# Third dense tap and paired image halves in a chain of four convolution blocks

## The reference

```python
# block 0: masked, grouped (4 groups)
out = relu(_gconv(x * m1, w1, 0))                 # 1x1, 256 -> 64
out = relu(_gconv(out * m2, w2, 1)) * m2          # 3x3, 64 -> 64
x = relu(_gconv(out, w3, 0) + x)                  # 1x1, 64 -> 256
# block 1: modulated deformable convolution
out = relu(group_norm(conv(x, w1)))               # 256 -> 64
om = conv(out, w_off, pad=1) + b_off              # 27 maps: 9 dx, 9 dy, 9 mask
sampled = bilinear_sample(out, py, px) * sigmoid(mask)    # 9 taps per pixel
out = einsum("bckhw,ock->bohw", sampled, w2)
out = relu(group_norm(out))
x = relu(group_norm(conv(out, w3)) + x)
# block 2: the same with biases in place of the norms and without modulation (18 maps)
# block 3: theta, phi, g = 1x1 of x to 16 channels (plus biases)
f = theta^T phi / N;  y = f g;  wy = conv1x1(y, w_w)
out = batch_norm(wy) + x
```

## Time and profile before

| | us |
|---|---|
| median of 3 runs (264.29 to 270.0) | 269.53 |
| the profiled execution | 269.83 |
| its span | 268.0 |
| busy: PE, DVE, ACT, POOL | 210.7, 158.3, 117.9, 136.0 |
| granted TensorE clock, mean | 0.877 of full |

### The profile page before, as it was taken

The page is one execution under the profiler, slowest core; times in us unless marked ns, Lnnn a source line. Parts: engine busy times, 40 slices in busy tenths (PEclk is TensorE's granted clock), DMA queues, the critical chain, the costliest instruction groups (busy, mean ns, idle before and its releaser), DMA issues. The chain is left out here.

```text
span 268.0 us, 2403 instructions
## 1 busy us (share of the span) xinstructions
PE 210.7 (79%) x808; PEld 109.6 (41%) x808; DVE 158.3 (59%) x270; ACT 117.9 (44%) x159; POOL 136.0 (51%) x127
## 2 busy tenths in 40 slices
PE   8999987787979568196997979489876764999920
PEld 7364963543333223034873746233332231343500
DVE  2965537766867954844166466567476676352271
ACT  2120335786686837001206148848738551023231
POOL 6000017877878877870010077788777787720010
PEclk9999995678899999677799975979899998699965
DMA  7400113323233232230000223223323223310004
GB/s 257 171 0 2 39 41 98 98 86 93 80 99 93 83 98 80 79 98 21 0 2 0 78 66 110 78 83 95 98 78 97 81 80 97 100 39 0 0 0 157
DMA packets 8654, 19.80 MB, mean 74 GB/s; under 512 B 1985, under 2 KB 4162, under 8 KB 8514
## 3 DMA queue, kind: packets, MB, share of 16 engines
q0 software_dynamic: 5376, 14.69, 18.0%
q1 hardware_dynamic: 3122, 4.44, 4.8%
q10 hardware_dynamic: 144, 0.52, 0.5%
HBM read 17.55 MB, written 2.10 MB: 73 GB/s over the span
## 5 line engine op out<-in xcount | busy, mean ns | idle before, releaser
L321 POOL DMA_INDIRECT G<-table,idx x112 | 129.1, 1153 | 58.1 <-issue 47.7
L558 DVE TENSOR_TENSOR GW<-G,corner_w 128x1024 f32<-128x1024 f32 (+1 forms) x32 | 34.9, 1091 | 52.0 <-DMA G<-table,idx 51.1
L951 PE MATMUL ps<-first,GS 128*128 128x128 f32 x64 | 15.5, 328 | 37.1 <-DVE GS L573 37.0
L753 ACT ACTIVATE sT<-ps 128x256 f32<-128x256 f32 x32 | 12.2, 381 | 64.0 <-PE ps L951 64.0
L906 PE MATMUL ps<-x,V 128*64 128x512 f32 x64 | 38.4, 731 | 0.0
L723 ACT ACTIVATE near_y<-ps,dbias 128x1024 f32<-128x1024 f32 x32 | 35.4, 1106 | 1.5 <-PE ps L898 1.5
L308 POOL TENSOR_TENSOR rstd<-var,half_neg 64x1 f32<-64x1 f32 (+1 forms) x4 | 2.6, 638 | 64.0 <-DVE var L371 42.2
L726 ACT ACTIVATE hat_y<-near_y 128x1024 f32<-128x1024 f32 x32 | 33.8, 1057 | 1.0
L799 PE MATMUL ps<-first 128*128 128x128 f32 x180 | 28.6, 316 | 0.0
L799 PEld LDWEIGHTS ps<-first 128*128 128x128 f32 x180 | 25.7, 224 | 4.2 <-issue 3.9
L951 PEld LDWEIGHTS ps<-first,GS 128*128 128x128 f32 x64 | 7.1, 153 | 45.0 <-DVE GS L573 43.7
(11 more groups left out here) (132 smaller groups left out, 235.1 us busy)
## 6 DMA issues: line engine op xcount, KB each, us to landing
G<-table,idx POOLq DMA_INDIRECT x112, 2.9
second<-in_second SPq DMA_DIRECT2D x1, 1552.5 KB, 8.6
table<-feat_t SPq DMA_DIRECT2D x4, 256.0 KB, 2.3
out<-x SPq DMA_DIRECT2D x4, 256.0 KB, 2.2
x<-in_x ACTq DMA_DIRECT2D x1, 512.0 KB, 4.6
x<-in_x SPq DMA_DIRECT2D x1, 512.0 KB, 5.4
first<-in_first SPq DMA_DIRECT2D x1, 224.0 KB, 4.4
at_w<-in_w_b SPq DMA_DIRECT2D x1, 1.0 KB
```

The lines of the kernel that those rows point to most:

```text
L321: pool.indirect_dma_start(out=G[:, done % RING, k, :], out_offset=None, in_=table[b], in_offset=bass.IndirectOffsetOnAxis(ap=idx[b][:, n:n ...
L558: dve.tensor_tensor(GW[:, :, k0:k1].rearrange("p c k e -> p k c e"), G[:, (b * TILES + t) % RING, k0:k1].rearrange("p k (c e) -> p k c e", ...
L753: act.activation(sT[:, t % 2, 2 * part:2 * part + 2], ps[:, B_ST[part], 0:2 * P] .rearrange("p (q n) -> p q n", n=P), ACT.Copy).then_inc(s ...
L951: mm = pe.transpose(ps[:, B_ST[part], q % 2 * P:(q % 2 + 1) * P], GS[:, t % 2, k:k + 2, :].rearrange("p k e -> p (k e)"), ident)
```

## The change

Nine taps are split 3 dense and 6 gathered. The second part of a tile has two taps, one pair, so 48 gathers a layer. A dense chunk isn't |.| then 1-|.| then times hat_x, but one `scalar_tensor_tensor`, min(|y distance|, 1) * hat_x; since hat_y = 1 - min(|.|, 1), the contribution is VS·hat_x - V·S, where VS is the sum of V over the tiles. So V is stored negated, and for each tap one matmul pair with VS is added. Line 726 goes; near_y becomes the ring, of 4. V of the third tap is in bank 7.

The 64-channel results of half 0 stand in partitions 0 to 63 and those of half 1 in 64 to 127 of one bank (`side(h)`): conv1, dense and contraction write the two halves to different columns of the array, conv3 reads them from different rows. hid is 128x512. conv3 waits for both halves; QUARTERS is ordered by slab, and the norms of 64 channels read 128 partitions in one bn_stats.

```diff
-DENSE = 2
+DENSE = 3
+PART_PAIRS = [range(0, 2), range(2, PAIRS)]
-BESIDE = [0, 0, 1, 1, 2, 1, 1, 2, 1, 1, 2, 1, 1, 2, 0, 0]
+BESIDE = [0, 0, 2, 1, 3, 2, 2, 2, 2, 2, 2, 2, 2, 1, 1, 0]
-PREPARE = [(-1, -1, -1), (3, FIRST_TAP_ENDS - AHEAD, 5)]
-HRING = 3
+PREPARE = [(-1, -1, -1)] + [(end - AHEAD - 1, end - AHEAD, end - AHEAD) for end in TAP_ENDS]
+HRING = 4
...
-        hid = 3 * [sb("hid", [HID, N])]
+        hid = 3 * [sb("hid", [P, HALF])]
...
+        def side(h):
+            return slice(h * HID, (h + 1) * HID)
...
-        QUARTERS = [(h, m) for h in range(2) for m in range(CT)]
+        QUARTERS = [(h, m) for m in range(CT) for h in range(2)]
+        OUT_QUARTERS = [(h, m) for h in range(2) for m in range(CT)]
... DVE
+            def weigh(b):
+                dve.wait_ge(s_V, 3 * b + 3)
+                dve.tensor_scalar(V2[:].rearrange("p t e -> p (t e)"), ps[:, B_V2, :], -1.0, None,
+                                  ALU.mult).then_inc(s_weigh, 1)
+                dve.tensor_reduce(VS[:, 2], ps[:, B_V2, :].rearrange("p (t e) -> p e t", e=HID),
+                                  mybir.AxisListType.X, ALU.add).then_inc(s_weigh, 1)
+                dve.tensor_scalar(V[:].rearrange("p t d e -> p (t d e)"),
+                                  ps[:, B_V:B_V + 2, :].rearrange("p h n -> p (h n)"), -1.0, None,
+                                  ALU.mult).then_inc(s_weigh, 1)
+                dve.tensor_reduce(VS[:, 0:2].rearrange("p d e -> p (d e)"),
+                                  ps[:, B_V:B_V + 2, :].rearrange("p h (t e) -> p e (h t)", e=2 * HID),
+                                  mybir.AxisListType.X, ALU.add).then_inc(s_weigh, 1)
...
-                    dve.wait_ge(s_hy, cd + 1)
+                    dve.wait_ge(s_ny, cd + 1)
...
-                    dve.tensor_tensor(S[cd % SRING], hat_y[cd % HRING], hat_x[:, c // TILES],
-                                      ALU.mult).then_inc(s_S, 1)
+                    dve.scalar_tensor_tensor(out=S[cd % SRING], in0=near_y[:, cd % HRING], scalar=1.0,
+                                             in1=hat_x[:, c // TILES], op0=ALU.min,
+                                             op1=ALU.mult).then_inc(s_S, 1)
... ACT
-                act.wait_ge(s_ny, cd + 1)
-                act.activation(hat_y[cd % HRING], near_y[:, c % 2], ACT.Relu,
-                               scale=-1.0, bias=1.0).then_inc(s_hy, 1)
... PE
             def conv1(b, weights, src, ready):
-                for h in range(2):
-                    for t in range(CT):
-                        pe.wait_ge(ready[t], h + 1)
-                        mm = pe.matmul(ps[0:m, B_C1 + h, :], weights[:, t, :], half(src[:, t, :], h),
+                for t in range(CT):
+                    for h in range(2):
+                        pe.wait_ge(ready[h], t + 1)
+                        mm = pe.matmul(ps[side(h), B_C1, :], weights[:, t, :], half(src[:, t, :], h),
                                        start=(t == 0), stop=(t == CT - 1))
...
             def conv3(b, weights, start):
-                for h in range(2):
-                    pe.wait_ge(s_hid[b], h + 1)
-                    for m in range(CT):
-                        pe.matmul(quarter(m, h), weights[:, m * P:(m + 1) * P], half(hid[b], h),
+                pe.wait_ge(s_hid[b], 2)
+                for m in range(CT):
+                    for h in range(2):
+                        pe.matmul(quarter(m, h), weights[side(h), m * P:(m + 1) * P], hid[b][side(h)],
                                   start=start, stop=True).then_inc(s_c3[b], 1)
... positions
+                                if i == 0:
+                                    pe.wait_ge(s_weigh, 4 * b + 2)
... dense(c)
+                    i, t = divmod(c, TILES)
+                    if t == 0:
+                        if c == 0:
+                            pe.wait_ge(s_weigh, 4 * b + 4)
+                        for h in range(2):
+                            pe.matmul(ps[side(h), B_C1, :], VS[:, i, :], half(hat_x[:, i], h),
+                                      start=(c == 0), stop=False)
                     for h in range(2):
-                        mm = pe.matmul(ps[0:HID, B_C1 + h, :], V[:, c % TILES, c // TILES, :],
-                                       half(S[(b * CHUNKS + c) % SRING], h), start=(c == 0),
+                        mm = pe.matmul(ps[side(h), B_C1, :], V2[:, t, :] if i == 2 else V[:, t, i, :],
+                                       half(S[(b * CHUNKS + c) % SRING], h), start=False,
```

More of the change, by code:

```diff
@@ L41 @@
 LAG = 2
-BESIDE = [0, 0, 1, 1, 2, 1, 1, 2, 1, 1, 2, 1, 1, 2, 0, 0]
+BESIDE = [0, 0, 2, 1, 3, 2, 2, 2, 2, 2, 2, 2, 2, 1, 1, 0]
 RESIDUAL = [1, 0, 1, 2]
 AHEAD = 2
-FIRST_TAP_ENDS = [sum(BESIDE[:u + 1]) >= TILES for u in range(UNITS)].index(True)
-PREPARE = [(-1, -1, -1), (3, FIRST_TAP_ENDS - AHEAD, 5)]
-HRING = 3
+TAP_ENDS = [[sum(BESIDE[:u + 1]) >= n * TILES for u in range(UNITS)].index(True) for n in (1, 2)]
+PREPARE = [(-1, -1, -1)] + [(end - AHEAD - 1, end - AHEAD, end - AHEAD) for end in TAP_ENDS]
+HRING = 4
 SRING = 4
@@ L153, in conv_chain @@
         mod_x = m0
-        near_y = sb("near_y", [P, 2, N])
-        hat_y_ring = sb("hat_y", [P, HRING, N])
-        hat_y = [hat_y_ring[:, n] for n in range(HRING)]
+        near_y = sb("near_y", [P, HRING, N])
         S_own = sb("S", [P, N])
         S = [S_own[:], x0[:, 0, :], x0[:, 1, :], mask[:]]
-        sT = sb("sT", [P, 2, PAIRS + 1, P])
+        sT = sb("sT", [P, 2, PAIRS, P])
         st = sb("st", [P, CT, 2, 6])
@@ L441, in _ @@
                                        half(m0[0:HID], h), ALU.add))
-                dve.scalar_tensor_tensor(out=half(hid[0], h), in0=half(m0[0:HID], h), scalar=0.0,
+                dve.scalar_tensor_tensor(out=hid[0][side(h)], in0=half(m0[0:HID], h), scalar=0.0,
                                          in1=half(mask[0:HID], h), op0=ALU.max,
@@ L523, in modulate, with taps_and_corners @@
                 dve.wait_ge(s_hxm, i + 1)
[L525 to L533 removed]
+            def taps_and_corners(b):
                 def product(c):
@@ L651, in _ @@
             for q, (h, m) in enumerate(QUARTERS):
-                if not m:
+                if not h:
                     act.wait_ge(s_c3[0], q + 1)
@@ L740, in phi_g @@
                 act.wait_ge(s_tpg, h + 1)
-                act.activation(half(pgT, h), ps[2 * D:4 * D, B_C1 + h, :], ACT.Copy).then_inc(s_pgT, 1)
+                act.activation(half(pgT, h), ps[2 * D:4 * D, B_TPG[h], :], ACT.Copy).then_inc(s_pgT, 1)
             def samples(b):
@@ L762, in _ @@
             act.wait_ge(s_sb, 2)
-            for h in range(2):
-                act.activation(half(hid[1], h), ps[0:HID, B_C1 + h, :], ACT.Relu,
-                               scale=sc[0:HID, 0:1], bias=nb[0:HID, 0:1]).then_inc(s_hid[1], 1)
+            act.activation(hid[1][:], ps[:, B_C1, :], ACT.Relu,
+                           scale=sc[:, 0:1], bias=nb[:, 0:1]).then_inc(s_hid[1], 2)
             for q, (h, m) in enumerate(QUARTERS):
@@ L782, in _ @@
             for h in range(2):
-                act.activation(half(th[0:D], h), ps[0:D, B_C1 + h, :], ACT.Identity,
+                act.activation(half(th[0:D], h), ps[0:D, B_TPG[h], :], ACT.Identity,
                                bias=fld["thb"][0:D]).then_inc(s_th, 1)
@@ L866, in last_conv3 @@
                 pe.wait_ge(s_hid[2], h + 1)
-                pe.matmul(quarter(m, h), fld["b2w3"][0:HID, m * P:(m + 1) * P], half(hid[2], h),
+                pe.matmul(quarter(m, h), fld["b2w3"][side(h), m * P:(m + 1) * P], hid[2][side(h)],
                           start=False, stop=True).then_inc(s_c3[2], 1)
@@ L877, in deform @@
                                        feat[:, (4 * h + t) * P:(4 * h + t + 1) * P],
-                                       dense_weights[0:HID, :], start=True, stop=True)
+                                       dense_weights[0:HID, 0:2 * HID], start=True, stop=True)
                     mm.then_inc(s_V, 1)
+                if b:
+                    pe.wait_ge(s_ny, CHUNKS)
+                for t in range(TILES):
+                    mm = pe.matmul(ps[:, B_V2, t * HID:(t + 1) * HID], feat[:, t * P:(t + 1) * P],
+                                   dense_weights[0:HID, 2 * HID:], start=True, stop=True)
+                mm.then_inc(s_V, 1)
                 def positions(u):
@@ L919, in contract @@
                     for q in pairs(u):
-                        mm = pe.matmul(ps[0:HID, B_C1 + t // 4, t % 4 * P:(t % 4 + 1) * P], w[:, q, :],
-                                       sT[:, t % 2, q], start=False, stop=(u == UNITS - 1 and q == PAIRS))
+                        mm = pe.matmul(ps[side(t // 4), B_C1, t % 4 * P:(t % 4 + 1) * P], w[:, q, :],
+                                       sT[:, t % 2, q], start=False, stop=(u == UNITS - 1 and q == PAIRS - 1))
                     if u == UNITS - 1:
@@ L1119, in pairs, with both @@
         w = w.reshape(HID, HID, TAPS).transpose(2, 1, 0)[:GTAPS]
```

(5 more changed lines are left out.)

122 lines of the change are left out of this document (58 added, 64 removed).

## The result

The changed kernel takes **247.59 us** (median of 4 runs, 247.54 to 248.84) against 268.68 for the kernel before, measured beside it (264.29 to 270.00): a ratio of 0.930, 95% interval 0.924 to 0.936. The forecast was 250.0, with a range of 244 to 261. A median counts every run, while a ratio leaves out executions that were disturbed, so it isn't the quotient of the medians.

A forecast was written before the change was run, and what follows sets the result against it. POOL issuing 56 gathers in a row was taken to bound both stages. Stages 16.2, their ends 1.7, head 1.65 and between 0.3 sum to 19.85 us off 269.83: 250.0 us, 8-in-10 range 244 to 261.

The forecast's parts named there:

- The bound, and 16 gathers off the path: Both gather stages: 8 of 56 gathers removed per stage at 1.245 us each, 9.96 us, all on the path.
- The lengthening: Gather stages: gathers grow longer while DVE works, 0.21 to 0.22 us per us; 13.5 and 13.4 us per stage.
- DVE's sum: Gather stages: DVE's added work, priced from rows, +9.0 us in the first and +7.9 in the second.
- DVE keeps up: Gather stages: a tile's DVE work, 7.8 us or 9.0 with a modulation, against 9.4 of gathers; five-tile ring absorbs the latter.
- rival A: Gather stages: DVE's added work takes back more, shown by DVE waiting on near_y or PE; 257.2 or 260 us; chance 0.20.
- Both stages are POOL issuing: Gather stages before the change: POOL issues 56 gathers in a row, 81.4 us; everything else there is cover.
- Between the stages: Behind the first gather stage: -0.9 us at the stage's end, -0.3 from four bn_stats running back to back.
- The 1.8 us that I had left out of the sum: PE's clock keepers behind the stage: 3.78 us at the lower clock, about 1.9 at full; counted only in the range.
- The head: Before the first gather: conv3 starts at 19.3, staggered pairs end at 23.6 against 25.25, -1.65 us.
- perfect sharing: Head: conv3 and conv1 pairs sharing the array fully, not staggered by one row, -2.5 us.
- Rival B: Halves don't share the array, so PE bounds the gather stages: 274.7 to 283.3 us, taken as 279; chance 0.08.
- The tail: Behind the second stage's last gather: smaller GW, GA, GS, one transpose and one contraction less, -0.8 us.

The follow-up runs named there:

- experiment 1: Changed kernel with a seventh, unread gather per tile: 268.55 us, ratio 1.000; and the kernel before with 11 gathers fewer: 253.86 us, ratio 0.939.
- the repetition: Changed kernel measured again, unaltered, as a control: 251.08, 247.21, 251.44 and 255.24 us, median 251.26.
- short_third: Changed kernel with DVE's products of the third dense tap cut to 2 of 1024 columns: 251.03 us, ratio 0.933.
- experiment 8: Kernel before with 4 of the 8 idle matmuls behind the first gather stage removed: 268.75 us, ratio 1.002.
- Experiment 2: Changed kernel with a one-column full-array matmul between the two halves of each dense chunk: 259.96 us, ratio 0.967.
- the two one-input kernels: Changed kernel with every product replaced by a one-input minimum, over 1023 columns: 287.09 us; over 1024 columns: 284.51 us.
- sum_on_pe: Changed kernel with the second corner addition moved from DVE to PE as two identity matmuls: 287.32, 256.26, 250.28 and 311.47 us, no ratio given.
- mod_early: Changed kernel with the modulation of the second and third tap prepared one unit earlier: 248.34 us, ratio 0.917.

## Why the prediction was right, step by step

**The bound, and 16 gathers off the path.** Right, and shown from both sides (experiment 1): the whole 21 us go with the 16 gathers.

**The lengthening.** 13.5 and 13.4 us were forecast; measured 58.05 - 48 x 0.945 = 12.7 for 62.3 us of DVE work, and 60.02 - 45.36 = 14.7 for 58.6. The first is 0.20 us per us of DVE, the second 0.25; the repetition had 10.5 (for 60.0 us of DVE work) and 14.8 (for 58.5). As a mean over both the slope of before holds (27.3 against 26.9), for a single stage it is good to 3 us. That is the whole miss of -8.95 and -6.97 against -8.1. The parts of DVE's sum were right, though its busy time rose by 14.2 us in all, not by the 16.9 of both stages: product 1217 ns (1218 forecast), tensor_reduce on the strided PSUM view 1213 for 1024 elements, GW of two taps 692 (686), mean gather 1230 (1220).

**DVE keeps up: only just, and not in the first stage.** Here a sign that the forecast named for rival A is in the trace, and yet not its price. Timeline of the changed kernel, first stage: PE, ACT, POOL, DVE.

```profile
64.33 0.79 PE L909 MATMUL ps<-om_split,sel 128*128 128x512 f32 x1 [2.46 <-ACT near_y L735]
...
67.22 1.22 PE L909 MATMUL ps<-om_split,sel 128*128 128x512 f32 x2
...
68.11 1.27 ACT L719 ACTIVATE m<-ps,dbias 128x512 f32<-128x512 f32 x2 [3.67 <-PE ps L909]
69.27 2.12 ACT L735 ACTIVATE near_y<-ps,dbias 128x1024 f32<-128x1024 f32 x2
...
69.41 0.94 POOL L329 DMA_INDIRECT G<-table,idx  x1 [0.30 <-issue]
...
70.47 1.23 DVE L558 SCALAR_TENSOR_TENSOR mask<-near_y,hat_x 128x1024 f32<-128x1024 f32 x1 [5.34 <-ACT near_y L735]
```

The position matmuls for the second tap ran at 1.2 GHz (0.72 us apart instead of 0.43), ACT waited for them with the modulation, near_y behind it, and DVE behind that. From there to its last sum at 112.9 DVE is busy for 40.3 of 42.4 us, and its GW at 109.11 starts without waiting. In the repetition the last gather ended 2.3 us sooner (107.01 instead of 109.35), and the first statistics behind the stage began at 114.08 instead of 114.22. So in the first stage DVE ends the chain, not POOL, as rival A had it; it costs little, since both end at nearly the same time. That it costs so little is luck: the argument for it had the ring absorb a slower tile, not two queues that end together. The step "Both stages are POOL issuing" was right to the end for the second stage alone. Why the 17 us of DVE work that short_third saves brought nothing has two parts: late results of PE, and the clock (its first statistics came 1.5 us sooner, but the keepers behind them took 3.50 us instead of 2.05).

**Between the stages: the step that was mis-sized, -3.89 instead of -1.2.** The row of keepers that stood at 3.78 us, and the statistics behind them:

```profile
114.12 2.05 PE L808 MATMUL ps<-first 128*128 128x128 f32 x16
...
120.26 2.90 DVE L603 BATCH_NORM_STATS2 st<-ps 128x6 f32<-128x512 f32 x4 [2.15 <-PE ps L826]
```

The 1.8 us that I had left out of the sum came, as the clock was at 2.4 GHz here; the granted clock of the stretch rose from 0.90 to 1.00, while that of the stages fell from 0.85 to 0.81 and 0.82. Last gather to first statistics fell from 6.15 to 4.87 us (-1.28, -0.9 forecast), hid as one activation gave 0.27, the four bn_stats in a row 0.37 (0.3 forecast). The prediction had it in the range and not in the sum. As a saving in the kernel before (experiment 8) it didn't move the total, so that it came in full here can't be counted on.

**The head: right sum (-1.61, -1.65 forecast), wrong picture.** Conv3 of the second half, then conv1, answering to the earlier trace rows:

```profile
19.95 1.99 PE L826 MATMUL ps<-hid,w3bd 64*128 64x512 f32 x8 [1.35 <-DVE hid L450]
21.87 1.94 PE L814 MATMUL ps<-x,second 128*64 128x512 f32 x8
```

Eight rows take 1.94 us where they took 3.65. The pair isn't staggered by a row: the records of two column halves start 6 to 7 ns apart (107.215 and 107.222, then 107.695 and 107.702), those of two row halves 36 ns (20.458 and 20.494), the next pair 0.43 us on. That is perfect sharing, priced at -2.5, but hid came 0.55 us later than I had put it, so that conv3 began at 19.95 rather than 19.3.

**Rival B** did not occur: the pairs in the rows settle it. Its price remains open. Experiment 2 added some 14 us to PE for each of the two layers, just under the "about 15 us of added PE work" at which it was to decide, and lengthened not the stages but what stands behind them. **The tail**, -0.9 against -0.8.

## What to carry to other kernels

Where one engine issues descriptors back to back, count its issues and price each with what other engines do to it; then look which engine ends last when the count falls: here DVE already did in the first stage. Judge a gain of 1 or 2 us only against a repetition of the same kernel, and by the fastest executions as well as the median: here the repetition alone moved the median by 3.7 us and the fastest by 0.3. Read an edit that is to keep two things apart back from the rows: here the second half of a chunk found a new partner. A chain in fixed order over PE, ACT and DVE beside uninterrupted gathers should be read for copies that start long after the matmul they wait for; in four kernels here, less work on the engine that slowed the gathers went with more of them.

## What the runs showed of the hardware

- **PE's signals late beside gathers.** With gathers every 1.25 us and DVE waiting, ACT began up to 34 us after the recorded end of the matmuls it waited for (normally within 0.05 us), and a wait and a fill of 0.29 us behind each gather took this from 58 us in all to 0. The longest rows of gathers at that spacing were 13, 17 and 14 in the two one-input kernels and sum_on_pe, 10 in short_third, and at most 7 in all others. ACT's part is ruled out by the semaphores' times; whether the matmuls themselves end late or only their signals is open, since the trace models the ends of matmuls. Whether the spacing decides, or that POOL waits between gathers for its own fill, is open too. A pause in the changed kernel itself, and in the one with the sum on PE, wasn't tried.
- **Two fp32 matmuls in different columns or rows of the array** start 6 to 36 ns apart and run together: 0.43 us for two of 512 columns. Two of different chunks did so as well, when nothing stood between them.
- **The granted clock** was 0.81 and 0.82 in the stages of the changed kernel, 0.85 in those before, and 0.83 and 0.93 with the one-column matmuls. That packing lowers it isn't shown: mod_early, with the same packed work, had 0.88 and 0.86.
- **Gathers and DVE:** a gather took 945 ns beside an idle DVE and 947 beside DVE rows that read PSUM, and 1.06 to 1.58 us beside the products and corner work of the kernel before.
- **DVE:** a tensor_scalar with one SBUF input over 1023 columns took 692 ns, over 1024 690 to 705, against 1217 for two inputs. A cast over 128x1152 took 1352 ns, one over 128x768 561.
